# Moving a third's overflow work and transposes ahead of its up products on TensorE

## The chip, the cores and the metric

The kernel runs on one core of one Trainium2 chip. The metric is the device time of one execution in microseconds (us). Three runs of the kernel before took 2498.66, 2502.98 and 2503.08 us; their median, 2502.98 us, is the time before.

## What is computed

The input is 1024 tokens of 512 features (32 sequences of 32). Three residual blocks follow: a cross attention over a context of 257 rows, a self attention, and a mixture of experts. The change lies wholly in the third one. Cut to what matters, the reference does this there:

```python
x = layernorm(x)                                  # 1024 tokens x 512
gates = softmax(x @ wg.T)                         # 64 experts
w_topk, idx_topk = top_k(gates, 8)                # 8 experts per token, weights normalised
# expert e gets its tokens in order, at most CAPACITY = 160 of them
buf[e, rank] = x[token]
h = buf @ expert_w1.T                             # 160 x 512 @ 512 x 3072
x1, x2 = split(h)                                 # "up" and "gate", 1536 each
out = (x1 * silu(x2)) @ expert_w2.T               # 160 x 1536 @ 1536 x 512
combined[token] += weight * out[rank]
```

A shared expert of the same width is added for all tokens. Everything is float32; TensorE's large products are made by splitting each operand into a high and a low part and adding three products.

## The kernel before

**Tiles.** An expert's 1536 hidden columns are worked on in three thirds of 512. A third is called n, from 0 to 191; its expert is e = n // 3 and its place in the expert is b = n % 3. Three weight units of 128 x 2048 float32 (1 MB) belong to a third: GATE, UPPER and DOWN. The first 128 tokens of an expert are worked on as a full tile. The up to 32 tokens beyond them are its overflow, worked on only where an expert has more than 128 tokens. Such an expert is called wide here, and the others narrow. `narrow` holds a 1 for each narrow expert, and `pe.If(now < 1)` skips the overflow code of the present expert where it is narrow (`before` is the same value for the last expert).

**Streams.** SyncE (`block.sync`, line 1418) loads the units into a ring of 10 places in a fixed order. Before a place is loaded again it waits until its last unit is used up: a DOWN unit by `d_done` (line 1422), a GATE or UPPER unit by `t_done`, which the transposes of line 1677 raise (line 1424). ScalarE copies each unit to its high part (`high`, line 1439), VectorE subtracts to make its low part (`low`, line 1519). Five units can be held in split form: `high` of unit k waits until TensorE has used unit k - 5 in the order of `SPLITS` (line 1407). So the high copy of GATE n + 2 waits for the up products of third n.

**TensorE.** Its order is written out by hand from line 1711 on. For third n:

- at b = 1, `turn_tokens(e + 1)`: five transposes for the next expert's tokens;
- `gates_of(n)`: 12 products of 512 columns with GATE n (lines 1627 to 1629);
- `uppers_of(n)`: 12 products with UPPER n (the same lines);
- overflow, if any: `over_down(n - 2)`, `over(n)` and `over_turn(n - 1)` (lines 1690, 1658, 1668), with branches at lines 1723 and 1728;
- `turn(n - 1)`: four transposes of the last third's activations (line 1677);
- `down(n - 2)`: 12 products with DOWN n - 2 (lines 1705 to 1707).

`turn(n)` waits for `gtl_done`, which is raised by `turned_low(n - 1)` on VectorE (line 1547), because both use the same bank of PSUM.

**ScalarE and VectorE.** Both work strictly in the order in which their loops issue. In iteration n ScalarE does, after `weigh` (b = 2) or the token copies (b = 1): `high` of UPPER n + 1, `silu(n)` (line 1447), `high` of DOWN n - 1, `high` of GATE n + 2, `silu_over(n)` (line 1457), `copy_turned(n - 1)` (lines 1464, 1465). VectorE does: `low` of UPPER n + 1, `low` of DOWN n - 1, `product(n)` (line 1527), `low` of GATE n + 2, `product_over(n)` (line 1534), `turned_low(n - 1)` (line 1547).

**GpSimd** gathers the tokens of expert e + 2 and adds the weighted results of expert e - 1 to the output by indirect DMAs.

Of the kernel before, what the change touches and what calls it, by code (L numbers as in the profile page):

```python
# [120 lines left out]
def program(nc, x, ctx_k, ctx_v, wq, wk, wv, wo, bq, bk, bv, bo, wg, shared, experts, out):  # L121
    root = ExitStack()
    with root:
# [5 lines left out]
        def sem(name):  # L129
            return root.enter_context(nc.semaphore(name))  # L130
# [26 lines left out]
        with ExitStack() as st:  # L157
# [46 lines left out]
            @block.sync  # L204
            def _(sp):
                for i in range(4):
                    sp.dma_start(X[:, 2 * i:2 * i + 2, :], x_dram[:, 2 * i:2 * i + 2, :]).then_inc(x_in[i], 16)

                def keys(b):

                    if b >= 4:
                        sp.wait_ge(s_done, 2 * (b - 3))
                    sp.dma_start(K[:, b % 4, :, :], ctx_k[b]).then_inc(k_in[b % 4], 16)

                def context(b):

                    if b >= 4:
                        sp.wait_ge(pv_done, b - 3)
                    sp.dma_start(V[0:KC, b % 4, 0:2, :], ctx_v[b, 0:2 * KC, :].rearrange("(k p) d -> p k d", p=KC)).then_inc(v_in[b % 4], 16)
                    sp.dma_start(V[0:KR, b % 4, 2, :], ctx_v[b, 2 * KC:SK, :]).then_inc(v_in[b % 4], 16)  # L220

                for b in range(4):
                    keys(b)
                    context(b)
                for b in range(B):
                    if b + 4 < B:
                        keys(b + 4)
                    if b >= 4:
                        context(b)
                for i, w in enumerate((wq, wk, wv, wo)):  # L230
                    sp.dma_start(W[:, i, :, :], w).then_inc(w_in, 16)
                for i, v in enumerate((bq, bk)):
                    sp.dma_start(bqk[:, i, :], v).then_inc(w_in, 16)
                for i, v in enumerate((bv, bo)):
                    sp.dma_start(bvo[:, i, :], v.to_broadcast([P, D])).then_inc(w_in, 16)
# [527 lines left out]
        lo_done = sem("e_lo_done")  # L763
# [25 lines left out]
        def source(i):  # L789

            kind, n = ORDER[i]
            return experts[n // NB, n % NB, kind]
# [560 lines left out]
        with ExitStack() as st:  # L1353
# [19 lines left out]
            def unit(i):  # L1373

                at = SLOTS[i % R]
                if at < RING:
                    return ring[:, at * UNIT:(at + 1) * UNIT]
                return more[:, (at - RING) * UNIT:(at - RING + 1) * UNIT]
# [32 lines left out]
            NTH = {u: i for i, u in enumerate(SPLITS)}  # L1411
# [4 lines left out]
            @block.sync  # L1416
            def _(sp):
                for i in range(RING, 3 * NP):
                    if i >= R:
                        kind, n = ORDER[i - R]  # L1420
                        if kind == DOWN:
                            sp.wait_ge(d_done, n + 1)
                        elif n >= 1:
                            sp.wait_ge(t_done, n)
                        else:
                            sp.wait_ge(u_done, 1)
                    sp.dma_start(unit(i), source(i)).then_inc(unit_in[i % R], 16)
# [178 lines left out]
            def _(pe):  # L1606
                def turn_tokens(e):

                    token_ps, overtoken_ps = turned_tokens(e)
                    pe.wait_ge(gathered[e % 2], 32 * (e // 2 + 1))  # L1610
                    pe.wait_ge(xel_done, e)
                    pe.wait_ge(xeo_done, e)
                    for k in range(G):
                        pe.transpose(token_ps[:, k * P:(k + 1) * P], XG[:, e % 2, k * P:(k + 1) * P], ident[:, :])  # L1614
                    if e >= 2:
                        pe.wait_ge(gto_done, NB * (e - 1))
                    pe.transpose(overtoken_ps, XO[:, e % 2, :], ident[:, :]).then_inc(xe_psum, 1)  # L1617

                def project(dst, kind, n, done):

                    e = n // NB
                    high, low = halves(NTH[kind, n])
                    pe.wait_ge(lo_done, NTH[kind, n] + 1)
                    for k in range(G):
                        h, l = XEh[:, e % 2, k, :], XEl[:, e % 2, k, :]
                        wh, wl = high[:, k * D:(k + 1) * D], low[:, k * D:(k + 1) * D]
                        pe.matmul(dst, h, wh, start=(k == 0), stop=False)  # L1627
                        pe.matmul(dst, h, wl, start=False, stop=False)  # L1628
                        last = pe.matmul(dst, l, wh, start=False, stop=(k == G - 1))  # L1629
                    last.then_inc(done, 1)  # L1630

                def gates_of(n):

                    if n % NB == 0:
                        pe.wait_ge(xel_done, n // NB + 1)
                    if n >= 1:
                        pe.wait_ge(silu_done, n)
                    project(gate_ps, GATE, n, g_done)

                def uppers_of(n):  # L1640

                    if n >= 1:
                        pe.wait_ge(gf_done, n)
                    project(up_ps, UPPER, n, u_done)

                def over(n):

                    e = n // NB
                    i = place(UPPER, n)
                    pe.wait_ge(unit_in[i % R], 16 * (i // R + 1))  # L1650
                    pe.wait_ge(xeo_done, e + 1)
                    if n >= 1:
                        pe.wait_ge(gfo_done, n)
                    for kind in (GATE, UPPER):
                        w = unit(place(kind, n))
                        for k in range(G):
                            for c in range(4):
                                pe.matmul(over_ps[32 * c:32 * c + 32, kind * P:(kind + 1) * P], XEo[:, e % 2, k, :],  # L1658
                                          w[:, k * D + c * P:k * D + (c + 1) * P], start=(kind == GATE and k == 0),
                                          stop=(k == G - 1), skip_group_check=True)  # L1660

                def over_turn(n):

                    pe.wait_ge(gfo_done, n + 1)
                    if n >= 1:
                        pe.wait_ge(gto_done, n)
                    pe.wait_ge(xeo_done, min(n // NB + 2, NE))
                    pe.transpose(overturn_ps, GFo[:, :], ident[:, :])  # L1668

                def turn(n):  # L1670

                    pe.wait_ge(gf_done, n + 1)
                    if n >= 1:
                        pe.wait_ge(gt_done, n)
                        pe.wait_ge(gtl_done, n)
                    for j in range(G):
                        last = pe.transpose(turn_ps[:, j * P:(j + 1) * P], GF[n % 2][:, j * P:(j + 1) * P], ident[:, :])  # L1677
                    last.then_inc(t_done, 1)
# [32 lines left out]
                for e in range(NE):  # L1711
                    now = pe.value_load(narrow[0:1, e:e + 1], min_val=0, max_val=1)
                    for b in range(NB):
                        n = NB * e + b
                        if b == 1 and e + 1 < NE:
                            turn_tokens(e + 1)
                        gates_of(n)
                        if n == 0:
                            with pe.If(now < 1):
                                over(n)  # L1720
                        uppers_of(n)
                        if b < 2 and n >= 2:
                            with pe.If(before < 1):
                                over_down(n - 2)
                                if b == 0:
                                    over_turn(n - 1)
                        if n >= 1:
                            with pe.If(now < 1):
                                over(n)
                                if b == 2:  # L1730
                                    over_down(n - 2)
                                if b >= 1:
                                    over_turn(n - 1)
                            turn(n - 1)
                        if n >= 2:
                            down(n - 2)
                    before = now
# [64 lines left out]
```

## Time and profile before

| | |
|---|---|
| median of 3 runs | 2502.98 us (2498.66 to 2503.08) |
| span of the profiled execution | 2494.3 us |
| median less span | 8.7 us |
| TensorE busy | 2406.8 us, 96% |
| VectorE busy | 1981.7 us, 79% |
| ScalarE busy | 1689.3 us, 68% |
| mean granted TensorE clock | 0.988 |
| DMA traffic | 715.08 MB, mean 287 GB/s |

The profile is of one execution on the core. No time of its own from outside is given for that execution, so its span is set against the median of the runs; the 8.7 us between them lie around the span, before its first and after its last instruction. Busy shares are of the span. The expert block runs from about 559 us to the end of the span; what is before it is not touched by the change. Starts of instructions are measured and the ends of matmuls are modelled, so that matmuls in a row overlap in the records: the distance from start to start is the pace.

### The profile page before, as it was taken

Reading aid. Unit: us, or ns where it says so; the run is one execution under the profiler, and the core shown is the slowest. Engines: PE = TensorE matmul, PEld = TensorE weight load, DVE = VectorE, ACT = ScalarE, POOL = GpSimd, SP = SyncE. Lnnn points to the kernel's source line nnn. Section 1 sums busy time; section 2 is a strip of 40 time slices with the busy share of each in tenths; the row PEclk is TensorE's granted clock in tenths of the full one; section 3 lists DMA queues with packets and bytes.
Section 4 is the critical chain, followed back from the end, with each engine's and each line's share of the span. In section 5 each row is a group of like instructions: output and inputs, shape, how many; then the busy total and the mean of one; then the engine's idle time right before and its main releaser. Section 6 shows DMA issues by size and latency. Waiting matters only on the chain.

```text
span 2494.3 us, 54951 instructions
## 1 busy us (share of the span) xinstructions
PE 2406.8 (96%) x22810; PEld 1959.0 (79%) x22810; DVE 1981.7 (79%) x1894; ACT 1689.3 (68%) x2121; POOL 569.7 (23%) x410
## 2 busy tenths in 40 slices
PE   6779989999999999999999999999999999999998
PEld 4557777778888888888888888888888888888886
DVE  7785667657899899988878989988778878877795
ACT  5553443336888788878777878877667767766784
POOL 0000020002223232332222223322222222212221
PEclk9989999999999999999999999999999999999999
DMA  8760042347999899999988999999888888878894
GB/s 231 217 212 1 3 168 88 112 160 271 360 378 383 325 374 388 384 340 361 343 307 318 386 341 363 371 353 353 285 311 324 322 300 328 324 275 285 328 359 135
DMA packets 129043, 715.08 MB, mean 287 GB/s; under 512 B 15488, under 2 KB 23808, under 8 KB 52928
## 3 DMA queue, kind: packets, MB, share of 16 engines
q1 hardware_dynamic: 103104, 668.06, 69.7%
q0 software_dynamic: 25600, 41.96, 7.9%
q8 instruction: 279, 4.57, 0.7%
q14 instruction: 60, 0.49, 0.1%
HBM read 684.46 MB, written 25.49 MB: 285 GB/s over the span
## 4 chain that ended last, share of the span: by engine, by line
PE 77%; issue 0%; POOL 0%; DVE 0%; ACT 0%; ACTq 0%; POOLq 0%; DVEq 0%
PE ps L1627 14%; PE ps L1629 14%; PE ps L1628 14%; PE ps L1705 7%; PE ps L1707 7%; PE ps L1706 7%; PE ps L1658 5%; PE ps L1677 4%; PE ps L1690 3%; PE ps L1614 1%; PE ps L1668 1%; PE ps L1617 0%; POOL out_rows L1590 0%; POOL out_rows L1588 0%; DVE e_XEl L1541 0%
## 5 line engine op out<-in xcount | busy, mean ns | idle before, releaser
L1519 DVE TENSOR_TENSOR e_WL<-ring,e_WH 128x2048 fp32r<-128x2048 f32 x231 | 528.8, 2289 | 116.9 <-ACT e_WH L1439 114.9
L1519 DVE TENSOR_TENSOR XSl<-ring,XSh 128x2048 fp32r<-128x2048 f32 x229 | 524.1, 2289 | 106.8 <-ACT XSh L1439 104.8
L1439 ACT ACTIVATE e_WH<-ring 128x2048 fp32r<-128x2048 f32 x231 | 442.3, 1915 | 45.6 <-PE ps L1629 27.9
L1439 ACT ACTIVATE XSh<-ring 128x2048 fp32r<-128x2048 f32 x229 | 438.7, 1916 | 47.0 <-PE ps L1629 28.9
L1576 POOL TENSOR_TENSOR e_tick<-e_tick 128x1 f32<-128x1 f32 x126 | 111.9, 888 | 1301.7 <-ACT X L1487 1202.4
L1627 PE MATMUL ps<-e_WH,e_XEh 128*128 128x512 f32 x920 | 361.9, 393 | 0.0
L1629 PE MATMUL ps<-e_WH,e_XEl 128*128 128x512 f32 x920 | 358.6, 390 | 0.0
L1628 PE MATMUL ps<-e_WL,e_XEh 128*128 128x512 f32 x920 | 358.1, 389 | 0.0
L1519 DVE TENSOR_TENSOR e_WL<-e_more,e_WH 128x2048 fp32r<-128x2048 f32 x114 | 260.9, 2289 | 52.0 <-ACT e_WH L1439 51.0
L1627 PE MATMUL ps<-XSh,e_XEh 128*128 128x512 f32 x616 | 243.0, 394 | 4.6 <-DVE e_XEl L1541 4.6
L1629 PE MATMUL ps<-XSh,e_XEl 128*128 128x512 f32 x616 | 240.7, 391 | 0.0
L1628 PE MATMUL ps<-XSl,e_XEh 128*128 128x512 f32 x616 | 240.5, 390 | 0.0
L1439 ACT ACTIVATE e_WH<-e_more 128x2048 fp32r<-128x2048 f32 x114 | 218.4, 1915 | 23.7 <-PE ps L1629 14.3
L1629 PEld LDWEIGHTS ps<-e_WH,e_XEl 128*128 128x128 f32 x920 | 172.7, 188 | 36.6
L1628 PEld LDWEIGHTS ps<-e_WL,e_XEh 128*128 128x128 f32 x920 | 172.9, 188 | 34.8
L1627 PEld LDWEIGHTS ps<-e_WH,e_XEh 128*128 128x128 f32 x920 | 172.8, 188 | 34.6
L1705 PE MATMUL ps<-e_WH,e_GTh 128*128 128x512 f32 x460 | 191.1, 415 | 0.6 <-issue 0.6
L1707 PE MATMUL ps<-e_WH,e_GTl 128*128 128x512 f32 x460 | 181.0, 393 | 0.0
L1706 PE MATMUL ps<-e_WL,e_GTh 128*128 128x512 f32 x460 | 179.8, 391 | 1.1 <-issue 1.1
L1590 POOL DMA_INDIRECT out_rows<-X,lists x64 | 174.5, 2726 | 19.5 <-issue 19.5
L1447 ACT ACTIVATE X<-ps 128x512 f32<-128x512 f32 x192 | 115.2, 600 | 63.1 <-PE ps L1629 63.1
L1627 PEld LDWEIGHTS ps<-XSh,e_XEh 128*128 128x128 f32 x616 | 116.1, 188 | 28.4 <-DVE e_XEl L1541 4.8
(243 smaller groups left out, 4602.6 us busy)
## 6 DMA issues: line engine op xcount, KB each, us to landing
ring<-in_experts SPq DMA_DIRECT2D x462, 1024.0 KB
e_more<-in_experts SPq DMA_DIRECT2D x114, 1024.0 KB, 8.3
ring<-in_shared SPq DMA_DIRECT2D x12, 1536.0 KB, 6.2
a_K<-in_ctx_k SPq DMA_DIRECT2D x32, 514.0 KB, 4.9
a_V<-in_ctx_v SPq DMA_DIRECT2D x32, 384.0 KB
a_V<-in_ctx_v SPq DMA_DIRECT2D x32, 130.0 KB
X<-in_x SPq DMA_DIRECT2D x4, 512.0 KB, 5.3
xn_scratch<-ring SPq DMA_DIRECT2D x1, 2048.0 KB, 8.5
```

The costliest lines, as they stand in the source:

```text
L1439: act.activation(halves(nth)[0], unit(i), ACT.Copy).then_inc(hi_done, 1)
L1447: act.activation(SL[n % 2], gate_ps, ACT.Silu).then_inc(silu_done, 1)
L1519: dve.tensor_tensor(l, unit(place(kind, n)), h, ALU.subtract).then_inc(lo_done, 1)
L1576: pool.tensor_tensor(tick[:, :], tick[:, :], tick[:, :], ALU.add).then_inc(ticked, 1)
L1590: pool.indirect_dma_start(out4, bass.IndirectOffsetOnAxis(lists[:, 1, e, 1:2], 0), Y2, None, compute_op=ALU.add).then_inc(added, 16)
L1627: pe.matmul(dst, h, wh, start=(k == 0), stop=False)
L1628: pe.matmul(dst, h, wl, start=False, stop=False)
L1629: last = pe.matmul(dst, l, wh, start=False, stop=(k == G - 1))
L1658: pe.matmul(over_ps[32 * c:32 * c + 32, kind * P:(kind + 1) * P], XEo[:, e % 2, k, :], w[:, k * D + c * P:k * D + (c + 1) * P], start=(kin ...
L1705: pe.matmul(down_ps, h, wh, start=(b == 0 and j == 0), stop=False)
L1706: pe.matmul(down_ps, h, wl, start=False, stop=False)
L1707: last = pe.matmul(down_ps, l, wh, start=False, stop=(b == NB - 1 and j == G - 1))
```

## The change

In third n, for n of 1 and up, the up products move behind the overflow work and the transposes. The order becomes: gate products, overflow work, `turn(n - 1)`, up products, down products. Third 0 keeps its order. SyncE gets one more wait: since `t_done` no longer tells that the low part of the same third's UPPER unit has been used, it now also waits for `lo_done` of the unit whose place is loaded again. ScalarE's, VectorE's and GpSimd's programs stay as they were.

```diff
@@ -1422,6 +1422,7 @@
                             sp.wait_ge(d_done, n + 1)
                         elif n >= 1:
                             sp.wait_ge(t_done, n)
+                            sp.wait_ge(lo_done, NTH[kind, n] + 1)
                         else:
                             sp.wait_ge(u_done, 1)
                     sp.dma_start(unit(i), source(i)).then_inc(unit_in[i % R], 16)
@@ -1718,7 +1719,8 @@
                         if n == 0:
                             with pe.If(now < 1):
                                 over(n)
-                        uppers_of(n)
+                        if n == 0:
+                            uppers_of(n)
                         if b < 2 and n >= 2:
                             with pe.If(before < 1):
                                 over_down(n - 2)
@@ -1732,6 +1734,7 @@
                                 if b >= 1:
                                     over_turn(n - 1)
                             turn(n - 1)
+                            uppers_of(n)
                         if n >= 2:
                             down(n - 2)
                     before = now
```

## Rows read from the trace of the kernel before

**Rows 1.** Busy time of each engine in four stretches of the expert block, and their sum.

```profile
core 0: us, PE busy (x) PEld busy (x) DVE busy (x) ACT busy (x) POOL busy (x), PEclk, DMA share, GB/s
1000.00:1500.00 500.00, 499.85 (x3584) 411.14 (x3583) 429.48 (x326) 387.38 (x429) 148.52 (x102) 1.00 0.93 346
...
sum 1921.00, PE 1918.47 PEld 1578.24 DVE 1605.68 ACT 1450.51 POOL 542.91; mean PE 479.62 PEld 394.56 DVE 401.42 ACT 362.63 POOL 135.73
```

**Rows 2.** Waits from 560 to 2480 us: us in total, times, longest.

```profile
ACT e_SLo L1457 <- PE ps L1677: 100.1, 70, 2.5
...
PE ps L1706 <- issue: 1.1, 1, 1.1
...
PE ps L1677 <- DVE e_GTl L1547: 0.3, 1, 0.3
```

**Rows 3.** SyncE's own waits, the same stretch and columns.

```profile
SPq L1427 <- PE ps L1677: 1300.4, 186, 9.6
```

**Rows 4.** TensorE's timeline in a narrow third: start, us, line, tiles, shape, count.

```profile
1199.40 0.39 PE L1629 MATMUL ps<-e_WH,e_XEl 128*128 128x512 f32 x1
1199.62 0.39 PE L1627 MATMUL ps<-e_WH,e_XEh 128*128 128x512 f32 x1
...
1202.12 0.39 PE L1629 MATMUL ps<-e_WH,e_XEl 128*128 128x512 f32 x1
1202.35 0.60 PE L1677 MATMUL ps<-ident,X 128*128 128x128 f32 x4
1202.70 0.48 PE L1705 MATMUL ps<-e_WH,e_GTh 128*128 128x512 f32 x1
...
1205.33 0.39 PE L1707 MATMUL ps<-e_WH,e_GTl 128*128 128x512 f32 x1
1205.56 0.39 PE L1627 MATMUL ps<-XSh,e_XEh 128*128 128x512 f32 x1
...
1208.05 0.39 PE L1629 MATMUL ps<-XSh,e_XEl 128*128 128x512 f32 x1
```

**Rows 5.** ScalarE's timeline in the same third.

```profile
1199.82 0.60 ACT L1447 ACTIVATE X<-ps 128x512 f32<-128x512 f32 x1
1200.32 1.91 ACT L1439 ACTIVATE e_WH<-ring 128x2048 fp32r<-128x2048 f32 x1
1202.61 1.92 ACT L1439 ACTIVATE e_WH<-e_more 128x2048 fp32r<-128x2048 f32 x1 [0.38 <-PE ps L1629]
```

**Rows 6.** VectorE's timeline in the same third.

```profile
1202.26 2.29 DVE L1519 TENSOR_TENSOR e_WL<-ring,e_WH 128x2048 fp32r<-128x2048 f32 x1
1204.47 0.68 DVE L1527 TENSOR_TENSOR X<-X,ps 128x512 f32<-128x512 f32 x1
1205.07 2.28 DVE L1519 TENSOR_TENSOR e_WL<-e_more,e_WH 128x2048 fp32r<-128x2048 f32 x1
1207.27 0.28 DVE L1534 TENSOR_TENSOR e_GFo<-e_SLo,ps 128x128 f32<-128x128 f32 x1
1207.47 0.68 DVE L1547 TENSOR_TENSOR e_GTl<-ps,e_GTh 128x512 fp32r<-128x512 f32 x1
```

**Rows 7.** The timeline near the end, where transposes wait for VectorE.

```profile
2474.51 0.68 DVE L1547 TENSOR_TENSOR e_GTl<-ps,e_GTh 128x512 fp32r<-128x512 f32 x1
...
2475.34 0.63 PE L1677 MATMUL ps<-ident,X 128*128 128x128 f32 x4 [0.26 <-DVE e_GTl L1547]
```

**Rows 8.** TensorE's timeline: a wide third's overflow, then token transposes.

```profile
1211.09 1.95 PE L1658 MATMUL ps<-ring,e_XEo 128*32 128x128 f32 x64
...
1216.22 0.60 PE L1614 MATMUL ps<-ident,XG 128*128 128x128 f32 x4
1216.65 0.27 PE L1617 MATMUL ps<-ident,XO 128*128 128x128 f32 x1
1216.68 0.48 PE L1627 MATMUL ps<-e_WH,e_XEh 128*128 128x512 f32 x1
```

**Rows 9.** Line 1658 by itself: count, ns min/median/max, first and last start.

```profile
L1658 PE MATMUL ps<-ring,e_XEo x3616: 272/273/297, 563.9 to 2442.0; 128*32 128x128 f32 x191
...
L1658 PE MATMUL ps<-e_more,e_XEo x800: 272/273/297, 596.7 to 2430.3; 128*32 128x128 f32 x160
```

**Rows 10.** Line 1519, the low parts: count, ns min/median/max, first and last start.

```profile
L1519 DVE TENSOR_TENSOR e_WL<-ring,e_WH x231: 2280/2292/2317, 560.3 to 2471.5; 128x2048 fp32r<-128x2048 f32 x116
```

**Rows 11.** Line 1728, TensorE's branch: count, ns min/median/max, first and last start.

```profile
L1728 PEldq COMPARE_BRANCH  x191: 65/217/3957, 570.7 to 2467.5; - x191
```

**Rows 12.** DMA queues from 500 to 2480 us: packets, MB, share of 16 engines.

```profile
q8 instruction: 219, 3.59, 0.7%
```

## The prediction

> **What bounds the kernel now.** I read the table of stretches first, then the waits, then the timelines of a third. In the expert block TensorE is busy for 1918.47 of 1921.00 us [rows 1], at the full clock of 2.4 GHz (PEclk 1.00). The reader should see that only 2.5 us there are idle: nothing that another engine or a DMA does now holds TensorE up for longer. The waits say the same. TensorE waited 1.1 us for its own issue and 0.3 us once for VectorE [rows 2]. VectorE comes next, 1605.68 us or 84%, then ScalarE with 75%. So the bound is the number of TensorE's instructions times their pace. A change of order alone can take away at most the idle time, but it can add waits. What has to be found is how early each thing arrives that TensorE waits for, before and after.
>
> **The change part by part.**
>
> *TensorE's own work.* Nothing is added or removed: 36 products, four transposes and the overflow work per third. Its pace depends on what stands beside what. From the first gate product to the next third's is 24 products, four transposes, 12 products. Products follow each other every 0.227 us (1199.62 to 1202.12 is eleven of them). Behind the transposes the first product needs 0.32 us to the next, and twelve take 2.63 us from first to last start (1202.70 to 1205.33) instead of 2.50 [rows 4]. In the new order there is again one block of transposes per third, and again a block of 36 products between two of them (up, down, gate instead of down, gate, up). The penalty behind the transposes moves from the down products to the up products. The same holds for the overflow block of a wide third, 1.95 us with its changeovers [rows 8]. Sum: 0.
>
> *The release of the ring.* `t_done` comes one block of up products earlier, 12 x 0.227 = 2.7 us. SyncE waits for the transposes for 1300.4 us in all [rows 3], so loads do start 2.7 us earlier. The wait that is added, for `lo_done` of a unit, is long over by then: VectorE splits UPPER n during third n - 1, and GATE n before that. Queued behind that wait on SyncE are only further unit loads, in their old order. What the earlier loads are worth: neither TensorE nor ScalarE has a wait for a DMA in the block, and the most that anyone could win is the 2.5 us of idle TensorE [rows 1]. The other end is a loss by crowding, since the DMA share is 0.93. But the same bytes move in the same third, and I see no way from there to TensorE while ring places are filled a third or more ahead. Value: 0, bounds -2.5 and +1.
>
> *The transposes' wait.* Here is the price. `turn(n + 1)` cannot start until `turned_low(n)` is over. I write it for the third of rows 4 to 6, which starts its last gate product at 1199.40. ScalarE's silu starts at 1199.82 and the high copy of a DOWN unit at 1200.32. VectorE then has its low part at 1202.26, the product at 1204.47, the low part of a GATE unit at 1205.07, the overflow product at 1207.27 and `turned_low` at 1207.47, which ends at 1208.15. That is a chain of 8.75 us from the last gate product, with VectorE working without a gap from 1202.26 on [rows 4 to 6]. Today the next transposes come after the next up products: the last gate product of the next third starts at 1208.05, so they start near 1208.28 + 2.7 = 1211.0, and have 2.8 us to spare. In the new order they are due at 1208.05 + 0.23 = 1208.28, 0.13 us after VectorE ends. How long the hand-over takes is shown once: `turned_low` ends at 2474.51 + 0.68 = 2475.19 and the waiting transposes start at 2475.34, so 0.15 us [rows 7]. The transposes are then 0.02 us late. Because TensorE's queue runs empty at this wait, the block of four also takes 0.63 instead of 0.60 us [rows 4, 7]. I price one such place at 0.02 + 0.03 = 0.05 us.
>
> *The second chain.* The up products end later against the gate products, and the high copy of GATE n + 2 waits for them. New last up product: transposes at 1199.62, first up product 0.35 later, last one 2.63 after that, so 1202.60. The copy starts 0.49 after such a product (1202.12 to 1202.61) and takes 1.92: 1205.01. VectorE begins its low part at 1205.07 today [rows 4 to 6]. So this copy is ready 0.06 us before VectorE wants it. It does not lengthen the chain, but from here on the cycle transposes, up products, high copy, low part, `turned_low`, transposes has no slack either: 0.35 + 2.63 + 0.49 + 1.92 + (1208.15 - 1205.07) + 0.15 = 8.62 us, plus the few hundredths between ScalarE's end and VectorE's start, against a third of 1208.05 - 1199.40 = 8.65. A delay is therefore neither made up for nor piled up; each place pays its own 0.05.
>
> *How many places.* The overflow products are 3616 + 800 = 4416 [rows 9], 64 for a third [rows 8], so 69 thirds or 23 experts are wide and 41 narrow. In a wide third 1.95 us of overflow work stand ahead of the transposes. That covers this wait, and it covers `over(n + 1)`, which waits for `product_over(n)`, the step just before `turned_low`, and still has the next gate and down products, some 5.5 us, between it and the up products. At b = 1 the token transposes give 0.46 us (1216.22 to 1216.68 [rows 8]) of slack to the third before them. That leaves two places per narrow expert, less the one in front of a wide expert: of the 41, 13 are followed by a wide one (counted along the timeline of line 1658, whose first and last start are in [rows 9]) and one is the last, so 41 + 27 = 68 places. 68 x 0.05 = 3.4 us. Bounds of one place: 0, if the hand-over is as short where TensorE is still busy with the last gate product; and 0.15, if the whole hand-over of rows 7 comes on top, 10 us in all. I take 0.05, since it is the difference of two measured rows.
>
> *Start and end.* Third 0 is unchanged. Behind the last third the same transposes stand behind the same chain and pay the same 0.3 us as now. Sum: 0.
>
> *Sum.* Span 2494.3 + 3.4 = 2497.7. The median lies 8.7 us above the span; with it 2506.4. I say 2506.
>
> **The rivals.**
>
> *Rival 1, VectorE becomes the pace of narrow thirds (slower).* Three paths meet within 0.06 us in the new order: TensorE's own work, the chain from the silu, and the cycle through the high copy. If either of the latter is longer by 0.1 us than I read it, because a semaphore takes longer or because ScalarE's `weigh` pushes the silu back, all 68 places pay it: 6.8 us on top of 3.4, 2513. It decides as soon as the chain exceeds the third by more than 0.05 us. For it: VectorE shows no gap in the chain [rows 6]. Against it: the low part, the longest step of the chain, takes 2280 to 2317 ns in all its 231 cases [rows 10].
>
> *Rival 2, instruction fetches surface (slower).* TensorE's queue now hides the reading of its program. Line 1728's branch takes 0.217 us in the median but up to 3.957 [rows 11], and all that TensorE ever lost to issue in one piece was 1.1 us [rows 2]. In the new order the queue is empty at each of the 68 places. Program packets come 219 times in 1980 us [rows 12], about once per third. If one place in ten (my assumption) met such a read without cover, 7 x 3.96 = 28 us would be lost, 2534. Against it: the branch stands ahead of the wait, so that the sequencer would mostly read while it has to wait anyway. The Trainium skill (Advanced Engine Details and Errata, ISA Cache) says that a line of the instruction cache is 256 instructions; the 3.59 MB over 219 packets of rows 12 agree, 16 KB each. Its rule that only two lines are held would speak for this rival, since a skipped overflow block can jump over most of a line; no row here shows how many are held.
>
> *Rival 3, something is won (faster).* SyncE's wait of 1300.4 us [rows 3] ends earlier, and the transposed activations are ready long before the down products. But only 2.5 us of idle TensorE can be taken back, 2500.5. More would need a quicker pace of the products themselves, for which no row speaks.
>
> *Rival 4, nothing at all.* The hand-over is hidden behind the last gate product: 2503.
>
> **How the numbers follow.** The forecast, 2506, gets 0.42, and nothing at all 0.20; both are within 0.2% (5 us), which is about what a measurement of this kernel can tell from no change, though the upper half of the forecast reaches over that bound at 2508. Rival 1 gets 0.23, rival 2 0.06, rival 3 0.09. Slower by over 0.2%: rivals 1 and 2 and a small part of the forecast, 0.32. Faster by over 0.2%: 0.07, since rival 3 mostly stays within 0.2%. Within: 0.61. The range of 8 in 10 reaches from 2499, the idle time won back and the lowest of the three runs, to 2516, where the upper bound of a place (10 us) and a little of rival 1 are in.
>
> **What would show it.** Right: TensorE's waits for `turned_low` (line 1547) at line 1677 some 68 times, hundredths of a us each; narrow thirds of 8.65 to 8.75 us; wide thirds unchanged; ScalarE's 100.1 us of waiting for the transposes at line 1457 [rows 2] gone; the unit loads 2.7 us earlier against the third. Wrong: an idle TensorE of over 8 us in the block, with VectorE as releaser (rival 1) or issue (rival 2), or a TensorE busy time that differs by over 5 us, which would mean that the order changes the pace itself.

## The result and the profile after

| | before | after |
|---|---|---|
| median | 2501.02 us (4 runs) | 2541.96 us (4 runs, 2534.87 to 2547.76) |
| ratio | | 1.0152, 95% interval 1.0132 to 1.0171 |
| span of the profiled execution | 2494.3 us | 2546.0 us |
| first gate product of the expert block | 559.4 us | 566.0 us |
| from there to the end | 1934.9 us | 1980.0 us |

The median of before has one run more than the one ahead of the prediction, 2499.06 us. One run of the experiment overflow_alone (4160 us; its median would be 2525.98 us without it) and two of the kernel before (2683 and 4815 us) fell in a slower state of the chip, and no ratio below uses them.

The change made the kernel 1.5% slower. The forecast was 2506 us, at most 2516. The block itself grew by 45.1 us. The other 6.6 us of the difference of the spans lie ahead of it, in code that the change doesn't touch; the profiled execution of before was a quick one in that part (in the profiled executions of the ten experiments with branches the block starts between 560.9 and 567.3 us).

All line numbers of the changed kernel are one to three higher than before: products 1628 to 1630, transposes 1678, branch 1730, `turned_low` 1548.

The stretches of the expert block in the changed kernel, columns as in [rows 1]:

```profile
core 0: us, PE busy (x) PEld busy (x) DVE busy (x) ACT busy (x) POOL busy (x), PEclk, DMA share, GB/s
566.00:1000.00 434.00, 424.70 (x2704) 346.80 (x2705) 371.52 (x279) 332.49 (x367) 123.94 (x86) 0.98 0.93 342
1000.00:1500.00 500.00, 487.67 (x3319) 397.95 (x3321) 420.74 (x318) 373.64 (x416) 142.60 (x100) 0.99 0.93 339
...
sum 1964.00, PE 1932.86 PEld 1581.53 DVE 1616.69 ACT 1436.16 POOL 530.89; mean PE 483.22 PEld 395.38 DVE 404.17 ACT 359.04 POOL 132.72
```

In these stretches TensorE was idle for 2.5 us before and is now for 31.1 us, and its busy time is 14 us longer for the same instructions, with a granted clock under 1.00. Who ended the idle time stands in the waits, 560 to 2530 us (the wait for `e_XEl` is the one ahead of the block's first product and was there before):

```profile
PE ps L1678 <- issue: 23.4, 10, 3.5
...
PE ps L1628 <- DVE e_XEl L1542: 4.5, 1, 4.5
...
PE ps L1628 <- issue: 3.9, 3, 2.6
...
PE ps L1630 <- issue: 2.8, 2, 2.2
```

It is "issue", not VectorE: ten waits of up to 3.5 us ahead of the transposes, where the longest in all of before is 1.1 us [rows 2]. Six of the ten sit in the second third (b = 1) of a narrow expert. This is the longest, in third 40:

```profile
952.57 0.39 PE L1708 MATMUL ps<-e_WH,e_GTl 128*128 128x512 f32 x1
952.80 0.60 PE L1615 MATMUL ps<-ident,XG 128*128 128x128 f32 x4
953.23 0.27 PE L1618 MATMUL ps<-ident,XO 128*128 128x128 f32 x1
953.26 0.48 PE L1628 MATMUL ps<-e_WH,e_XEh 128*128 128x512 f32 x1
...
955.89 0.39 PE L1630 MATMUL ps<-e_WH,e_XEl 128*128 128x512 f32 x1
959.80 1.09 PE L1678 MATMUL ps<-ident,X 128*128 128x128 f32 x4 [3.53 <-issue]
960.54 0.78 PE L1628 MATMUL ps<-e_WH,e_XEh 128*128 128x512 f32 x1
961.12 0.63 PE L1629 MATMUL ps<-e_WL,e_XEh 128*128 128x512 f32 x1
961.54 0.63 PE L1630 MATMUL ps<-e_WH,e_XEl 128*128 128x512 f32 x1
```

The transposes were due at 956.1 and start at 959.80. After it the products follow at 0.43 us instead of 0.23. The clock of those stretches:

```profile
952.00:961.00 9.00, 5.47 (x27) 4.43 (x26) 8.24 (x6) 6.03 (x9) 0.00 (x0) 0.88 0.66 249
961.00:966.00 5.00, 5.00 (x14) 3.86 (x14) 0.03 (x1) 0.00 (x0) 0.00 (x0) 0.53 0.81 293
966.00:971.00 5.00, 5.00 (x24) 4.12 (x22) 3.73 (x4) 4.99 (x7) 0.96 (x2) 1.00 0.55 193
```

So TensorE idles 3.5 us and then works for 5.9 us at its lower level, 1.2 GHz (in the trace's record of the clock that level lasts from 958.85 to 965.67, and begins within the gap). What it idles for is told by its sequencer's own row, the branch over the overflow code, in this window (count, ns min/median/max, first start), and by the DMA queues from 952 to 960 us:

```profile
L1730 PEldq COMPARE_BRANCH  x1: 5947/5947/5947, 953.7 to 953.7; - x1
```

```profile
q8 instruction: 1, 0.02, 0.8%
```

The branch began at 953.7, 2.4 us ahead of the transposes' time, and lasted 5.95 us instead of 0.2. Within it one program packet of 16 KB arrived (its transfer ran from 957.3 to 958.3, and the branch ended 1.4 us later). TensorE's queue held only gate products when the branch began, and ran out. In the kernel before, the same kind of branch met the same kind of read:

```profile
L1728 PEldq COMPARE_BRANCH  x1: 3820/3820/3820, 771.9 to 771.9; - x1
```

There the transposes were due at 775.67 and began at 775.84: of 3.8 us all but 0.17 was hidden, because the last gate products and the twelve up products behind them were still to be done.

Not every gap stands behind a long branch. In six of the eleven gaps of over 1 us (thirds 22, 39, 47, 55, 112 and 145) the branch rows are short, and the packet comes while the sequencer is in the code behind the branch. In third 55 the branch at 1096.79 took 0.22 us. The sequencer then waited for `turned_low` until 1098.52, handed over two of the four transposes and then stood still; the packet ran from 1100.03 to 1100.98:

```profile
1099.20 0.38 PE L1678 MATMUL ps<-ident,X 128*128 128x128 f32 x2
1102.36 0.69 PE L1678 MATMUL ps<-ident,X 128*128 128x128 f32 x2 [2.78 <-issue]
```

Over the whole block: distances between starts of over 0.7 us, each less 0.33, add up to 31.1 us in 16 places, against 1.9 in 2 places before; 23.1 of them at b = 1. Products at the low clock (0.43 us apart, 0.2 more than at the full one) cost another 11.0 us against 1.4. The two differences, 29.2 and 9.6 us, are 38.8 of the 45.1 us.

Where did the lead go? Lead is meant here as the time by which the sequencer, which hands the instructions over, is ahead of TensorE, which works them off. Two waits of the sequencer shorten it, at different points (medians over narrow thirds). One was priced in the prediction, `turned_low`. The sequencer passed this wait 2.8 us (b = 0 and 2) or 3.4 us (b = 1) before the transposes began, and now passes it 0.1 or 0.7 us before. This wait comes after the branch and does not change the lead there, which stays at 3.8 and 4.1 us for b = 0 and 2. The other wait was not seen, and it cuts the lead at the branch of b = 1, from 3.8 to 2.5 us: ahead of the last token transpose at b = 1 (line 1618) TensorE waits until ScalarE has copied the overflow transposes (`e_GTo`) out of the same bank. ScalarE's rows for the third above:

```profile
950.33 1.92 ACT L1440 ACTIVATE XSh<-ring 128x2048 fp32r<-128x2048 f32 x1 [2.96 <-PE ps L1630]
952.16 0.25 ACT L1458 ACTIVATE e_SLo<-ps 128x128 f32<-128x128 f32 x1
952.31 0.59 ACT L1465 ACTIVATE e_GTh<-ps 128x512 fp32r<-128x512 f32 x1
952.79 0.28 ACT L1466 ACTIVATE e_GTo<-ps 128x128 f32<-128x128 f32 x1
953.54 0.60 ACT L1473 ACTIVATE e_XEh<-ps 128x512 fp32r<-128x512 f32 x1 [0.48 <-PE ps L1618]
```

The copy ends at 953.07 and the transpose starts at 953.23. At 62 of the 63 such places in the changed kernel less than 0.3 us lie between the two, where before it was 1.9 us in the median. TensorE is not held up by it, but its sequencer is: it could queue the gate products only then, and came to the branch with 2.4 us of work in the queue. ScalarE sat idle for 2.96 us before, waiting for the up products, which the change made later against everything else.

The shorter lead is not the whole of it: the long reads are longer too. No branch of before took over 3.96 us; five take 5.0 to 6.0 us now. Third 40's gap is, as an estimate from these rows, some 1.4 us of lost lead (3.8 less 2.4) and 2.0 us of a longer read (5.95 against 3.96). The time goes by before the packet starts: 0.7 to 1.6 us from the branch's start before, 2.6 to 3.6 us at these five. At the four of them with b = 1, SyncE had issued a unit load 0.7 us before the branch, here at 952.99:

```profile
952.99 0.33 SPq L1428 DMA_DIRECT2D ring<-in_experts  x1
```

In before no load was issued in the last 1.1 us ahead of a long branch. Whether the load holds the packet up was not tested by itself.

### The profile page after: what moved, and what is told of

Read it like the earlier page. It is cut to its first block, busy times and chain, and to the rows that moved or that the text cites. A ratio compares the mean times of both kernels' runs of the same rounds, so it can differ in the third digit from the quotient of the medians.

```text
span 2546.0 us, 55328 instructions
## 1 busy us (share of the span) xinstructions
PE 2430.0 (95%) x22810; PEld 1969.5 (77%) x22810; DVE 1992.9 (78%) x1894; ACT 1674.6 (66%) x2121; POOL 558.7 (22%) x410
## 4 chain that ended last, share of the span: by engine, by line
PE 76%; issue 1%; DVE 0%; POOL 0%; ACT 0%; ACTq 0%; DVEq 0%; POOLq 0%
PE ps L1628 14%; PE ps L1630 14%; PE ps L1629 14%; PE ps L1706 7%; PE ps L1707 7%; PE ps L1708 7%; PE ps L1659 5%; PE ps L1678 4%; PE ps L1691 3%; PE ps L1615 1%; PE ps L1669 1%; PE ps L1618 0%; DVE e_WL L1520 0%; ACT e_WH L1440 0%; POOL out_rows L1591 0%
## 5 line engine op out<-in xcount | busy, mean ns | idle before, releaser
L1577 POOL TENSOR_TENSOR e_tick<-e_tick 128x1 f32<-128x1 f32 x126 | 125.3, 994 | 1366.5 <-ACT X L1488 1318.2
L1628 PE MATMUL ps<-e_WH,e_XEh 128*128 128x512 f32 x920 | 376.4, 409 | 0.6 <-issue 0.6
L1628 PE MATMUL ps<-XSh,e_XEh 128*128 128x512 f32 x616 | 252.1, 409 | 7.8 <-DVE e_XEl L1542 4.5
L1528 DVE TENSOR_TENSOR X<-X,ps 128x512 f32<-128x512 f32 x192 | 131.3, 684 | 114.4 <-PE ps L1630 112.9
L1706 PE MATMUL ps<-e_WH,e_GTh 128*128 128x512 f32 x460 | 179.1, 389 | 0.0
L1591 POOL DMA_INDIRECT out_rows<-X,lists x64 | 169.3, 2645 | 19.5 <-issue 19.5
```

Source lines behind the costliest of these rows:

```text
L1528: dve.tensor_tensor(GF[n % 2], SL[n % 2], up_ps, ALU.mult).then_inc(gf_done, 1)
L1577: pool.tensor_tensor(tick[:, :], tick[:, :], tick[:, :], ALU.add).then_inc(ticked, 1)
L1591: pool.indirect_dma_start(out4, bass.IndirectOffsetOnAxis(lists[:, 1, e, 1:2], 0), Y2, None, compute_op=ALU.add).then_inc(added, 16)
L1706: pe.matmul(down_ps, h, wh, start=(b == 0 and j == 0), stop=False)
```

## The experiments

Four theories stood. **Lead**: the sequencer's lead over the engine is what hides long instruction reads, and the change shortened it. **Loads**: the unit loads that start earlier crowd the reads. **VectorE**: the chain over `turned_low` paces TensorE (rival 1). The fourth, that something else about certain thirds is slow, came up with the places of the gaps. Each experiment was timed beside the kernel before on the same chip. "Gaps" and "low clock" below are the two sums as counted above, in the profiled execution.

| experiment | median us | ratio (95%) | gaps us | low clock us |
|---|---|---|---|---|
| changed kernel | 2541.96 | 1.0152 (1.0132 to 1.0171) | 31.1 | 11.0 |
| overflow_alone | 2532.27 | 1.0117 (1.0082 to 1.0152) | 16.8 | 5.2 |
| late_loads | 2558.17 | 1.0212 (1.0191 to 1.0234) | 42.4 | 16.6 |
| act_first | 2510.81 | 1.0038 (1.0025 to 1.0050) | 6.9 | 1.4 |
| copies_first | 2502.49 | 0.9999 (0.9985 to 1.0013) | 2.0 | 1.4 |
| two_banks | 2535.70 | 1.0119 (1.0094 to 1.0144) | 25.9 | 6.0 |
| short_lead | 2547.01 | 1.0176 (1.0142 to 1.0210) | 35.1 | 7.0 |
| lead_nine | 2544.08 | 1.0159 (1.0133 to 1.0185) | 30.5 | 10.0 |
| after_shift | 2540.86 | 1.0153 (1.0126 to 1.0179) | 26.8 | 5.8 |
| before_shift | 2501.09 | 0.9993 (0.9980 to 1.0006) | 2.0 | 1.6 |
| after_moved | 2545.41 | 1.0178 (1.0161 to 1.0195) | 28.3 | 6.4 |
| plain_before | 2291.56 | | 0.4 | 1.4 |
| plain_after | 2292.07 | | 1.1 | 1.6 |

**overflow_alone** moves the overflow work, but leaves the transposes behind the up products.

```diff
-                            turn(n - 1)
                             uppers_of(n)
+                            turn(n - 1)
```

> Only the overflow work is moved ahead of the up products; the transposes stay behind them, and SyncE has no added wait. Lead theory (TensorE's sequencer used to run ahead of the engine by some 3.4 us where it meets the branches, the change took that lead away at two waits, and now the 3 to 6 us that a branch sometimes waits for its instructions are seen, with a half-clock stretch behind the longest): the waits on turned_low and on the overflow copy are as far ahead as before, but the branches now have only gate products in front of them; normal branches hide, a few long ones show. 2500 to 2512 us, idle TensorE in the expert block under 10 us. Loads theory (earlier unit loads crowd the instruction reads): loads are as early as before, 2501. VectorE theory (the chain over turned_low paces TensorE): the transposes have their 2.8 us back, 2501.

Slower by 1.2%, more than any theory said. `turned_low` is over 2.9 us before the transposes here, as in the kernel before, so VectorE's chain is not needed for the loss, and SyncE's program is that of the kernel before. What is left is that the branches come one block of up products earlier in the program. The waits (560 to 2510 us) show reads again, now in front of the up products, where three waits for a low part seem to come in:

```profile
PE ps L1627 <- DVE XSl L1519: 6.1, 3, 2.8
PE ps L1629 <- issue: 5.1, 3, 2.2
...
PE ps L1627 <- issue: 3.9, 2, 2.1
```

The three are reads as well. The low part that those up products need had been ready for over 10 us. Each of the three times a long branch (2.4, 5.7 and 2.3 us) ended 0.2 us before the product started. This is the longest; it ended at 1421.09, and the product started at 1421.31:

```profile
L1729 PEldq COMPARE_BRANCH  x1: 5663/5663/5663, 1415.4 to 1415.4; - x1
```

Beside gaps and low clock some 6 us more were lost here in amounts of under 0.2 us, spread over nearly all thirds; where from is open.

**late_loads** gives the loads their old time.

```diff
-                            sp.wait_ge(lo_done, NTH[kind, n] + 1)
+                            sp.wait_ge(u_done, n + 1)
```

> The changed kernel, but SyncE waits for the up products (u_done) of the same third instead of lo_done, so that the unit loads start about as late as in the kernel before. Lead theory: nothing changes, 2535 to 2548 us, the long idle gaps of TensorE stay at thirds of b = 1. Loads theory: the instruction reads are quick again, back to 2501 to 2510.

Both expectations missed. That the earlier loads cause the loss is refuted: later loads make it worse, by 16 us. The gaps stand in nearly the same thirds (22, 40, 55, 64, 88, 112, 121 and 145 among them), but there are 20 instead of 16, and the longest branch takes 6.66 us instead of 5.95. That the loads have to do with the length of a read is not refuted. The four longest branches (5.4 to 6.7 us) again have a unit load issued 0.7 us before them, and their packets start 3.0 to 4.3 us after them. In after_shift and after_moved, below, three branches with a load as close before them waited only 1.2 to 1.8 us for their packet, so it is no rule, and no experiment takes it apart.

**act_first** gives back one of the two waits: ScalarE copies the transposed activations and the overflow before it makes the high part of GATE n + 2.

```diff
+                    silu_over(n)
+                    if n >= 1:
+                        copy_turned(n - 1)
                     if n + 2 < NP:
                         high(GATE, n + 2)
-                    silu_over(n)
-                    if n >= 1:
-                        copy_turned(n - 1)
```

> The changed kernel, but ScalarE does silu_over and copy_turned ahead of the high copy of GATE n + 2, so that the token transposes at b = 1 need not wait for the overflow copy; VectorE's order stays, and so does the transposes' wait for turned_low. Lead theory: the lead at the branch of b = 1 is back at some 3.4 us, and the gaps of b = 1, about 29 of the 45 us that the block grew by, mostly go; those of b = 0 and 2 stay: 2508 to 2522. Loads theory: no change, 2535 to 2548. VectorE theory: no change, 2535 to 2548.

31 of the 41 us come back, as the lead theory had it, with TensorE's and SyncE's programs untouched. The gaps at b = 1 shrink from 23.1 to 2.0 us. The lead at the branch of b = 1 is 3.2 us, up from 2.5, and the overflow copy ends 4.2 us before the token transpose in the median. The transposes still start 0.15 us after `turned_low` in 63 thirds, which acquits VectorE of nearly all the loss. The reads are short again too: no branch takes over 3.94 us, and no packet starts later than 1.6 us after its branch. So the experiment gives back both at once, lead and length, and does not say how much of the 31 us belongs to either.

**copies_first** does the same on VectorE (`product_over` and `turned_low` ahead of `low(GATE, n + 2)`).

> As act_first, and VectorE too does product_over and turned_low ahead of the low part of GATE n + 2. turned_low then ends some 2.4 us before the transposes are due. Lead theory: both waits are far ahead again, idle TensorE under 8 us in the block, 2498 to 2507. Loads theory: 2535 to 2548. VectorE theory: 2501, and the 0.15 us hand-over at line 1677 gone.

No difference from the kernel before can be measured. `turned_low` in a narrow third now comes right behind the products, and ends 2.3 us before the transposes:

```profile
1202.51 0.68 DVE L1528 TENSOR_TENSOR X<-X,ps 128x512 f32<-128x512 f32 x1
1203.11 0.28 DVE L1535 TENSOR_TENSOR e_GFo<-e_SLo,ps 128x128 f32<-128x128 f32 x1
1203.31 0.68 DVE L1548 TENSOR_TENSOR e_GTl<-ps,e_GTh 128x512 fp32r<-128x512 f32 x1
1203.91 2.28 DVE L1520 TENSOR_TENSOR XSl<-ring,XSh 128x2048 fp32r<-128x2048 f32 x1
```

Long reads there are as many as ever; the branch's row still has one of 4.3 us:

```profile
L1730 PEldq COMPARE_BRANCH  x191: 65/217/4343, 573.6 to 2472.5; - x191
```

TensorE lost no more than 0.6 us in one piece to any of them (560 to 2490 us):

```profile
PE ps L1678 <- issue: 1.3, 4, 0.6
...
PE ps L1628 <- issue: 0.7, 2, 0.5
```

**two_banks** takes away the other wait alone: the transposes of the middle third go to another bank, so that those at b = 2 and b = 0 need not wait for the last `turned_low`.

```diff
+            def turn_of(n):
+
+                return ps[:, 6 if n % NB == 1 else 2, :]
...
-                    if n >= 1:
-                        pe.wait_ge(gt_done, n)
-                        pe.wait_ge(gtl_done, n)
+                    if n % NB == 1:
+                        pe.wait_ge(xel_done, min(n // NB + 2, NE))
+                    read = n if n % NB == 0 else n - 1
+                    if read >= 1:
+                        pe.wait_ge(gt_done, read)
+                        pe.wait_ge(gtl_done, read)
```

> The changed kernel, but the transposes of a third with b = 1 go to another bank of PSUM (that of the token transposes), so that at b = 2 and b = 0 the transposes don't wait for the last turned_low; the wait of the token transposes for the overflow copy at b = 1 stays. Lead theory: the gaps of b = 0 and 2 (8.0 us) and the 0.15 us hand-overs go, those of b = 1 (23.1 us) and the half clock behind them stay: 2522 to 2538 us. VectorE theory: as before, 2502.

In the expected range; 17.5 of the 25.9 us of gaps are at b = 1. But 8.4 us stay at b = 0 and 2, where I had expected them to go, so this part of the expectation failed. The lead there is whole (3.8 and 4.1 us at the branch, and 3.4 us at the wait behind it, in narrow thirds), but some reads outlast it: the branch of third 63 took 5.2 us.

**short_lead** and **lead_nine** leave the old order and cut the lead directly. A semaphore is raised by the sixth (short_lead) or third (lead_nine) of the twelve up products, and the sequencer waits for it behind them.

```diff
                         last = pe.matmul(dst, l, wh, start=False, stop=(k == G - 1))
+                        if kind == UPPER and k == 1:
+                            last.then_inc(lead, 1)
...
                         uppers_of(n)
+                        pe.wait_ge(lead, n + 1)
```

> The kernel before, in its old order, with one thing added: behind the up products TensorE's sequencer waits until the sixth of the twelve up products is done, before it goes on to the branches. The six products that are left in the queue last 1.4 us, longer than the normal 0.2 us branches and the waits, so TensorE has no new wait of its own. Lead theory: the lead at line 1728 falls from 3.7 us to 1.3, and the eight branches of 3.1 to 4.0 us (27.9 us together) each show 2 to 3 us, plus a half-clock stretch behind some: 2515 to 2530 us. Loads and VectorE theories: the order of work is that of before, 2502.

> As short_lead, but the sequencer goes on when the third of the twelve up products is done, so nine are left, 2.0 us. If the loss goes by the lead, it is smaller than short_lead's 44 us and larger than 0: the lead at the branch is about that of the changed kernel at b = 1 (2.5 us), so 2515 to 2540 us. If short_lead's loss came from the added wait or from TensorE's semaphore update itself, it stays at 2547.

This is the test that the lead theory could have failed, since order, loads and both other engines' programs are as before. Both are slower, by as much as the changed kernel. The amounts were missed: short_lead lies 17 us above its expected range and lead_nine 4 us, and the two can't be told apart by their intervals. The median lead at the branch is 0.9 us in short_lead and 1.6 in lead_nine, less than I had taken. That lead_nine lost as much as short_lead is what the expectation had named for another cause, the added wait itself. The thirds rule that out. The wait stands in every third, but 16 thirds make up the whole loss of short_lead's block (42.8 us) and 15 that of lead_nine's (40.8 us); the others, some 175, differ from before by less than 0.3 us each and 0.3 us together. In both the reads moved from the branch to the code behind it, where the sequencer passes its wait only 0.4 to 0.7 us (short_lead) or 1.1 to 1.4 us (lead_nine) ahead of the transposes. The longest, in short_lead:

```profile
935.56 0.39 PE L1630 MATMUL ps<-e_WH,e_XEl 128*128 128x512 f32 x1
935.79 0.38 PE L1680 MATMUL ps<-ident,X 128*128 128x128 f32 x2
940.50 0.69 PE L1680 MATMUL ps<-ident,X 128*128 128x128 f32 x2 [4.33 <-issue]
```

Two of four transposes had been queued when the sequencer ran into the read.

**after_shift, before_shift, after_moved** ask whether the gaps belong to places in the program. A never-taken branch with 64 transposes in it is put into third 0:

```diff
+                        if n == 0:
+                            with pe.If(now < 0):      # after_moved: now > 0
+                                for i in range(64):
+                                    pe.transpose(turn_ps[:, 0:P], X[:, 0, 0:P], ident[:, :])
                         gates_of(n)
```

> The changed kernel with 64 transposes (128 instructions) in a branch of third 0 that is never taken: nothing of them is executed, but all later code lies half a block of 256 instructions further on. If the gaps come from instruction reads at the borders of such blocks, they move to other thirds than 22, 40, 55, 64, 88, 112, 121 and 145, and about as much is lost, 2525 to 2550 us. If they belong to what happens in those thirds (their loads, tokens or overflow), they stay there.

> The same never-taken branch in the kernel before. With 3.4 to 3.7 us of lead at the branches its long instruction reads stay hidden wherever they fall: 2500 to 2508 us.

> after_shift's branch turned out to be folded away, so that its program was the changed kernel's again but for a jump. Here the condition (now > 0) is kept in the program; the branch is not taken in third 0 of this data, and 64 transposes, 128 instructions, lie there unexecuted. If the gaps come from instruction reads at fixed distances in the program (16 KB, 256 instructions), most of them move to other thirds than 22, 40, 55, 64, 88, 112, 121 and 145, and the total stays at 2525 to 2550 us, or changes by as much as the new places lie better or worse. If they belong to what happens in those thirds, they stay there.

In after_shift and before_shift the program builder drops the body, since `now` can't be negative, so that they are repeats of the two kernels but for one jump. As such they say that the places repeat: after_shift has its eight largest gaps in thirds 22, 40, 55, 64, 88, 112, 121 and 145 once more. after_moved does hold the 128 instructions. Its gaps stand at 10, 19, 34, 43, 52, 67, 100, 109, 133 and others. Six of these are 22, 55, 64, 112, 121 and 145 less 12; 40 and 88 have no such partner, and 19, 34 and 67 are new. The tokens, loads and overflow of the thirds are the same, and what is lost is about the same too. So the places go with the program's layout. That the borders of the 16 KB packets set them fits, but is not shown.

**plain_before, plain_after** leave out the overflow work of all experts but the first, and with it the branches.

> The kernel before, with the overflow work of all experts but the first left out together with its branches, so that TensorE's program is one straight line with 88 to 98 instructions per third, and the rows of overflow tokens are not computed. All thirds are narrow: 193 thirds of 8.65 us and the token transposes. 1.95 us and more fall away for each of 66 thirds; about 2300 us. It is the measure for plain_after.

> The same left out of the changed kernel. The transposes wait for turned_low at some 125 places and the token transposes wait for the overflow copy at each b = 1, as in the changed kernel, but there is no branch and nothing to jump over. Lead theory: no long gaps; only hand-overs of 0.03 to 0.05 us, 4 to 6 us above plain_before. VectorE and loads theories: all thirds are narrow, so the loss is larger than in the changed kernel, 40 to 100 us above plain_before.

Without a branch the two orders cost the same as far as the medians tell: 2291.56 and 2292.07 us, and not 4 to 6 us apart as expected. The blocks of the two profiled executions are 1722.2 and 1726.9 us. If all of these 4.7 us go to the hand-over from `turned_low` at 125 transposes, it costs 0.04 us each. The prediction had put 0.05 on one place.

## Why the prediction was wrong

*From span to median.* I added 8.7 us to the span and said that they lie around it. They do not: the changed kernel's profiled execution took 2547.76 us with a span of 2546.0, 1.8 us more. The rest of the 8.7 us is that the profiled execution of before was quicker than the median. Beside the miss of 36 us this is small.

*TensorE's own work, sum 0.* Right at the full clock: plain_after's block is 4.7 us longer, and that takes in the hand-overs. What the low clock adds is below.

*The release of the ring, 0.* Outside the bounds of -2.5 and +1: late_loads shows that the earlier loads are worth 16 us in the new order. Its gaps are 11.3 us longer and its low clock costs 5.6 us more. How loads and reads of the program act on each other is open.

*The transposes' wait, 68 places of 0.05 us.* Right. Late starts are there: 60 of the transposes in the changed kernel begin less than 0.2 us after `turned_low`, at 0.147 us, as [rows 7] said, and the price per place is 0.04 us in the plain pair. In the changed kernel 170 of 191 thirds differ from before by less than 0.2 us each, 1.9 us together.

*The second chain.* The timing was right (in the third at 2440 us ScalarE's high copy ends at 2445.73 and VectorE's low part starts at 2445.77), but one user of ScalarE's copies was left out. `turn_tokens` at b = 1 waits for the overflow copy, and the copy now ends as the token transposes are due. By the prediction's way of counting it costs nothing, since TensorE does not wait; with the copy moved forward 31 us came back (act_first).

*The step that failed* is in rival 2: "the branch stands ahead of the wait, so that the sequencer would mostly read while it has to wait anyway". With it the sum for 2506 put reads of the program at nothing, and what happened got 0.06. The sequencer does meet the branch ahead of the wait, but the reads of over 3 us began only when it was there (0.7 us later at the least), and more program has to be read behind the wait. At b = 1 the overflow copy held it back until some 2.5 us were left at the branch, and the long reads took 3 to 6 us. Behind the wait for `turned_low` 0.1 to 0.7 us were left, and some reads fell there. The runs showed 31.1 us of gaps and 11.0 us at the low clock in its place. The sign named for rival 2, over 8 us of idle TensorE with issue as releaser, is what came. Rival 2's size, one place in ten of 68 at 3.96 us or 28 us, is close to the 29 us of gaps that were added, but by luck: there were 16 gaps of 1.9 us on average. Its sum left out the low clock behind the longer gaps, some 10 us more, since it priced a gap by its length alone. It also put the loss at the 68 places of `turned_low`, while 23.1 of the 31.1 us sat at b = 1. And it took the reads of before as they were, while the longest grew from 3.96 to 5.95 us. The evidence was in the rows: [rows 11] had a branch of 3957 ns where the median is 217, and [rows 2] showed that no more than 1.1 us of such a thing ever reached TensorE. What lay between was cover, and I did not ask what a smaller cover would show.

*Rival 1, VectorE.* Ruled out as the main cause by act_first (63 hand-overs, 0.4% slower) and by the plain pair. *Rivals 3 and 4* did not happen; copies_first is what rival 4 looks like, 2502.49 us.

No version measured here beats the kernel before. Where its long reads are hidden, at most some 2 us of idle TensorE are left to win.

## What to carry to other kernels

An engine without idle time may still live on its sequencer's lead. In this kernel cutting it, with the order left as it was, cost 1.6 to 1.8%. Before a wait is moved close to its due time, look for what the lead hides: the largest duration of the branches, not their median, and how many microseconds of queued work TensorE still has when each begins. The largest duration is no upper bound for the new order: here it grew by 2 us. If a reordering costs lead, move the producers' copies forward too (copies_first), so that every wait on the saturated engine is over well before its instruction is due.

## What the runs showed of the hardware

- TensorE's branch over up to some 200 instructions takes 0.2 us in the median, but over 1 us, up to 6.7 us, at eight to eleven of 191 places in every kernel with branches but short_lead (none) and lead_nine (one). In the kernel before and in the changed one a 16 KB packet of program falls into each branch of over 3 us: it starts 0.7 to 3.6 us after the branch does, takes 0.9 to 1.1, and the sequencer goes on 1.4 to 1.6 us after its end. The Trainium skill (Advanced Engine Details and Errata, Control Flow Timing) gives 108 ns for a compare-and-branch; the row here says 217 in the median and up to 5947 ns.
- After 3.5 us without work TensorE worked for 5.9 us at half the clock, in which eleven products lost 0.2 us each: about two thirds of the gap again.
- The eight largest gaps stood in the same thirds in the profiled executions of the changed kernel and of after_shift. With 128 unexecuted instructions put ahead (after_moved), six of the eight stood 12 thirds earlier.
